# Ending a feed-forward layer and starting attention: earlier weight loads, sums written in place, keys moved

## The chip, the cores and the metric

The kernel runs on one core of a Trainium2 chip. The metric is the device time of one execution in microseconds (us); lower is better. A change of less than about 0.2% (3 us) is not told apart from none here.

## The reference

A "macaron" layer over x of shape (8, 512, 256), 4096 rows in all, in 32-bit floats:

```
x = x + 0.5 * ffn(layernorm(x))      # first feed-forward
x = x + attention(layernorm(x))      # 16 heads of 16, causal, over 512 rows
x = x + 0.5 * ffn(layernorm(x))      # second feed-forward, same weights

ffn(x) = silu(x @ w1) * (x @ w2) @ w3          # shared, hidden size 1024
       + sum over the top 2 of 16 experts of sigmoid-gate * (silu(x @ e1) * (x @ e2) @ e3)
attention: q, k, v = x @ Wq.T, x @ Wk.T, x @ Wv.T; softmax(q k / 4, causal) v; @ Wo.T
```

## The kernel before

The rows are handled in 8 chunks of 512 rows (`CHUNK`). One function, `feed_forward`, is called twice: for the first layer with `exact` false, for the second with `exact` true. Products are made in parts: each factor is split in a rounded high part and the rest (low part), and three of the four products are added.

In the first feed-forward the shared part of chunks 0 to 5 (`BEHIND` = 6) is computed first (`chunks_before`) and its result goes to DRAM (`dram.sh`). Then come 80 blocks of 128 rows sorted by expert (`steps`, `NB` = 80). Each block's result is evicted by VectorE (DVE) into one of four buffers `yr` and scattered to `outputs_by_choice` in DRAM by an indirect DMA that GpSimd (POOL) issues (line 1163). POOL issues the scatter of block i only when that of block i-2 has landed. Last comes the shared part of chunks 6 and 7 (`chunks_behind`), 16 steps s = 0 to 15, one for each tile of 128 hidden columns. This text calls them step 0 to step 15. A step is on TensorE (PE) "up(s)", 12 matmuls of L1712, then "down(s-1)", 12 matmuls of L1726 and L1730. Between them ScalarE (ACT) makes silu (L1273) and the high part of the hidden tile (L1277), and DVE the hidden tile (L1548) and its low part (L1565). up(s) also needs the hidden tile of step s-2, and down(s) both parts of step s.

In the shadow of these 16 steps the parts of all 8 chunks are added up:

- SyncE (SP) loads chunk c's two expert outputs (`load_y`, 1 MB, one of four buffers `yg`) and, for chunks 0 to 5, the shared result (`load_acc`, 0.5 MB, one of four buffers `acc`).
- ACT scales the second expert output by its gate at step `SCALE_AT[c]` = 3, 4, 5, 7, 8, 9, 10, 12 (L1227, in `ahead`).
- DVE adds the first, gated, and then the scaled second (`combine`, L1634 and L1631) at steps `COMBINE_AT`: chunk 0 at 3 and 4, chunk 1 at 4 and 5, chunk 2 at 5 and 6, chunk 3 at 7 and 8, chunks 4, 5 and 6 both at 10, 11 and 12, chunk 7 at 13 and 14. The second raises the semaphore `summed`.
- SP stores the sum (`store_out`) to `dram.x1`, and when it has landed reuses the `acc` buffer.

The start of attention is drawn into the same steps. Chunk 0's sum, loaded back from DRAM into `att.x1[:, 1]`, gets its layer norm statistics on DVE (step 9), the deviation on POOL (semaphore `a_dev`), the normalisation on ACT (step 11, `a_normed`), and is turned on PE (the "turn", L1786, after up(12) and before down(11)). ACT and DVE split it in parts (steps 13 and 14), and PE projects it with the weights `att.wqk` (the "projection", L1804, after down(14)), which have to be loaded back from DRAM together with `att.wv` (`a_w_in`). The projections' parts are laid out by DMAs into `att.qT` and `att.kT`, whose rows POOL has cleared before (`a_clear`).

What sets the order of the work is the program text of each engine. Each engine runs its own list in order, and SP's DMAs go through one queue in order. The attention tiles lie over the same memory as `yg`, `acc` and the experts' weights. In units of 1024 floats for each partition, `yg` lies at 0 to 8, `acc` at 8 to 12, `xb` at 12 to 14, `att.x1` at 16 to 18, `att.wqk` and `att.wv` at 20.5 to 23.5. Before, `att.kT` was at 0 to 8 (four slots of 2) and `att.qT` at 8 to 12. SP's list at the point of the change:

```python
            for c in range(AN):
                load_acc(c)
            for r in range(4):
                sp.wait_ge(y_st[r], 16 * (NB // 4))      # all scatters have landed
            for c in range(3):
                load_y(c)
                if c == 0 and not exact:
                    sp.wait_ge(y_ld[0], 16)
```

Of the kernel before, what the change touches and what calls it, by code (L numbers as in the profile page):

```python
# [6 lines left out]
P = 128  # L7
F32 = mybir.dt.float32
F32R = mybir.dt.float32r
# [406 lines left out]
def attention_memory(z, m):  # L416
# [6 lines left out]
    a.kT = m.sb("kT", [P, KEEP, GROUP, CHUNK], F32R)  # L423
    a.qT = m.sb("qT", [P, KEEP, GROUP // 2, CHUNK], F32R)

# [90 lines left out]
def lay_keys(eng, sem, att, s, parts, part, r):  # L516

    src, k = parts[:, part, :].bitcast(F32), att.kT[:, s].bitcast(F32)
# [58 lines left out]
def feed_forward(nc, z, g, dram, tag, x_src, pre, post, out):  # L578
# [27 lines left out]
    with ExitStack() as ctx:  # L606
# [80 lines left out]
        else:  # L687
# [8 lines left out]
            a_x_in = m.sems("a_x_in", 2)  # L696
# [118 lines left out]
        def _(sp):  # L815
# [242 lines left out]
            for c in range(AN):  # L1058
                load_acc(c)
            for r in range(4):  # L1060
                sp.wait_ge(y_st[r], 16 * (NB // 4))
# [9 lines left out]
            if not exact:  # L1071
                sp.dma_start(att.wqk[:].bitcast(F32).rearrange("p h k g n -> p (h k g n)"), dram.wqk).then_inc(a_w_in, 16)
                sp.dma_start(att.wv[:].bitcast(F32).rearrange("p h k n -> p (h k n)"), dram.wv).then_inc(a_w_in, 16)
            for c in range(NC):
                sp.wait_ge(summed, c + 1)
                if not exact and c == NC - 1:

                    sp.wait_ge(a_clear, 2)
                    sp.wait_ge(acc_st[0], 32)
# [5 lines left out]
                if c < BEHIND:  # L1085
                    store_out(c, acc[:, c % AN], acc_st[c % AN])
                    if c + GS < NC:
                        load_y(c + GS)
                    if c + AN < BEHIND:
                        sp.wait_ge(acc_st[c % AN], 16)  # L1090
                        load_acc(c + AN)
                        if not exact:
                            sp.dma_start(att.x1[:, 1 - c], out[bass.ds(c * CHUNK, CHUNK), :]
                                         .rearrange("(t p) d -> p t d", p=P)).then_inc(a_x_in[c], 16)
# [7 lines left out]
            else:  # L1102
                sp.wait_ge(a_x_in[1], 16)
# [3 lines left out]
        def _(pool):  # L1107
# [59 lines left out]
            if not exact:  # L1167
# [10 lines left out]

                pool.wait_ge(a_var, 1)
# [8 lines left out]

                pool.wait_ge(summed, 6)
                pool.sem_inc(g.held, 1)  # L1190
                for s in range(2):
                    nc.gpsimd.memset(att.kT[0:ROWS, s].bitcast(F32), 0.0).then_inc(a_clear, 1)

                pool.wait_ge(summed, 8)
                pool.sem_inc(g.held, 1)
                for s in range(2, KEEP):
                    nc.gpsimd.memset(att.kT[0:ROWS, s].bitcast(F32), 0.0)

        @block.scalar
        def _(act):  # L1200
# [19 lines left out]
            def ahead(s):  # L1220

# [7 lines left out]
                if s == 11:  # L1230
                    act.wait_ge(a_dev, 4)
                    for t in range(CT):
                        ins = nc.scalar.activation(att.xn[:, t, :], att.x1[:, 1, t, :], ACT.Identity,
                                                   bias=att.veps[:, 0, t:t + 1], scale=att.rstd[:, 0, t:t + 1])
                    ins.then_inc(a_normed, 1)
                elif s == 13:
# [3 lines left out]
                elif s == 15:  # L1240
# [6 lines left out]
                    act.wait_ge(acc_st[0], 32)  # L1247
# [64 lines left out]
        def _(dve):  # L1312
# [274 lines left out]
            def ahead(s):  # L1587

                if s == 9:
                    dve.wait_ge(a_x_in[0], 16)  # L1590
# [25 lines left out]
            def combine(c, k):  # L1616
# [12 lines left out]
                if k == 1 and not exact:  # L1629
                    dve.wait_ge(y_scaled, c + 1)  # L1630
                    v.tensor_tensor(base, base, yg[:, c % GS, :, 1, :], ALU.add).then_inc(summed, 1)  # L1631
# [312 lines left out]
def attention(nc, z, g, dram, att, mine, own, pre):  # L1944
# [75 lines left out]
    with ExitStack() as ctx:  # L2020
# [85 lines left out]
        def _(sp):  # L2106
# [6 lines left out]
            def lay_out(G):  # L2113
# [3 lines left out]
                q, k = qT[:, s].bitcast(F32), kT[:, s].bitcast(F32)  # L2117
# [63 lines left out]
            for part in range(2):  # L2181
# [6 lines left out]
            sp.dma_start(kT[ROWS:LAST_ROWS].bitcast(F32).rearrange("p s (g a) n -> p (s g) (a n)", a=2),  # L2188
                         pick[:].rearrange("p (o a) n -> p o (a n)", o=1).to_broadcast([2, KEEP * HG // 2, 2 * CHUNK])
                         ).then_inc(ones_in, 16)  # L2190
# [46 lines left out]
            sp.wait_ge(ones_in, 16)  # L2237
# [74 lines left out]
        def _(act):  # L2312
# [12 lines left out]
            def high(G):  # L2325
# [5 lines left out]
                if G < AHEAD:  # L2331

                    hi, lo = hiT[:, G % 2, :].bitcast(F32), loT[:, G % 2, :].bitcast(F32)
                    q, k = qT[:, G].bitcast(F32), kT[:, G].bitcast(F32)
# [446 lines left out]
```

## Time and profile before

| | |
|---|---|
| time, median of 3 runs | 1507.82 us (1505.16 to 1508.35) |
| time of the profiled execution | 1503.83 us |
| its span, first to last instruction | 1501.6 us |
| PE busy | 1427.6 us, 95% of the span |
| DVE, ACT, POOL busy | 64%, 44%, 39% |
| mean granted TensorE clock | 0.981 of full |

### The profile page before, as it was taken

What the parts mean: (1) busy time and instruction counts of PE and PEld (TensorE: products, weight loads), DVE (VectorE), ACT (ScalarE), POOL (GpSimd) and SP (SyncE); (2) the same over time, 40 slices, a digit from 0 to 9 for tenths busy, and PEclk for the clock granted to TensorE, in tenths of its full rate; (3) what the DMA queues carried; (4) which work ended last, traced back from release to release, by engine and by line L of the source; (5) the groups of instructions that cost most, each with busy time, mean ns of one, the idle gap of its engine ahead of it and who ended that gap; (6) DMA issues with size and microseconds to landing.
All of it is one profiled execution on the core that took longest, in us unless ns stands there. A gap on an engine that the chain in (4) does not pass through costs nothing. (4 is left out here: it accounts for less than half of the span.)

```text
span 1501.6 us, 28710 instructions
## 1 busy us (share of the span) xinstructions
PE 1427.6 (95%) x8840; PEld 1168.7 (78%) x8840; DVE 960.5 (64%) x2045; ACT 662.1 (44%) x1347; POOL 585.6 (39%) x832
## 2 busy tenths in 40 slices
PE   5899999999989978999999999889999899999998
PEld 2688878888878866767777767658888788888887
DVE  5678855565545756777677767536786455555566
ACT  4534444334333443656665565553322244343332
POOL 6528820233323023464465454321288333333100
PEclk9999999999999998999999999989999999999999
DMA  9897998534396856345554555445464634356941
GB/s 342 309 342 270 329 342 345 180 105 144 104 318 211 284 160 147 92 115 143 144 142 119 129 123 134 140 157 201 169 244 145 225 103 148 104 199 209 312 127 57
DMA packets 176533, 285.80 MB, mean 190 GB/s; under 512 B 20738, under 2 KB 125698, under 8 KB 176146
## 3 DMA queue, kind: packets, MB, share of 16 engines
q1 hardware_dynamic: 134642, 206.31, 43.6%
q0 software_dynamic: 19104, 56.64, 10.3%
q10 hardware_dynamic: 22656, 21.11, 4.8%
q8 instruction: 81, 1.33, 0.4%
q14 instruction: 50, 0.41, 0.1%
HBM read 144.20 MB, written 109.84 MB: 169 GB/s over the span
## 5 line engine op out<-in xcount | busy, mean ns | idle before, releaser
L1712 PE MATMUL f_bank<-f_xparts,f_sw 128*128 128x512 f32 x1536 | 375.9, 394 | 3.9 <-DVEq L1642 3.4
L1712 PEld LDWEIGHTS f_bank<-f_xparts,f_sw 128*128 128x128 f32 x1536 | 282.6, 190 | 59.8 <-DVEq L1642 4.3
L1163 POOL DMA_INDIRECT outputs_by_choice<-f_yr,f_home x160 | 153.6, 960 | 361.4 <-DVE f_yr L1666 306.2
L2438 DVE TENSOR_REDUCE at_mx<-at_ps 128x2 f32<-128x512 f32 (+2 forms) x352 | 213.3, 632 | 91.9 <-PE at_ps L2574 80.2
L2323 ACT ACTIVATE at_pT<-at_ps 128x512 f32<-128x512 f32 (+1 forms) x352 | 190.5, 560 | 70.0 <-PE at_ps L2596 63.7
L2251 POOL TENSOR_SCALAR_AFFINE_SELECT at_pT<-at_pT 128x128 f32<-128x128 f32 (+2 forms) x352 | 123.8, 358 | 206.4 <-ACT at_pT L2323 201.3
L1121 POOL DMA_INDIRECT rows_by_slot<-f_xq,slot x128 | 146.3, 1143 | 123.8 <-issue 72.3
L1655 DVE TENSOR_TENSOR f_sil<-f_sil,f_bank 128x256 f32<-128x256 f32 x160 | 67.4, 421 | 165.0 <-ACT f_sil L1297 152.5
L1548 DVE TENSOR_TENSOR f_hid<-f_sil,f_bank 128x512 f32<-128x512 f32 x128 | 87.8, 686 | 132.0 <-PE f_bank L1712 103.3
L2596 PE MATMUL at_ps<-fa_qT,fa_kT 98*128 98x256 f32 (+3 forms) x512 | 162.3, 370 | 6.9 <-DMA fa_qT<-at_mT 3.5
L1277 ACT CAST f_hparts<-f_hid 128x512 fp32r<-128x512 f32 x128 | 79.4, 620 | 202.0 <-DVE f_hid L1548 192.7
L1726 PE MATMUL f_bank<-f_sw,f_hparts 128*128 128x256 f32 x1024 | 147.3, 287 | 3.8 <-ACT f_hparts L1277 2.1
L1726 PEld LDWEIGHTS f_bank<-f_sw,f_hparts 128*128 128x128 f32 x1024 | 139.0, 192 | 13.5 <-ACT f_hparts L1277 5.3
L2574 PE MATMUL at_ps<-fa_kT,fa_qT 96*128 96x256 f32 (+2 forms) x448 | 147.4, 367 | 1.8 <-DVE at_mx L2438 1.8
L1273 ACT ACTIVATE f_sil<-f_bank 128x512 f32<-128x512 f32 x128 | 76.3, 596 | 143.6 <-PE f_bank L1712 119.4
L1297 ACT ACTIVATE f_sil<-f_bank 128x256 f32<-128x256 f32 x160 | 61.6, 385 | 173.5 <-PE f_bank L1846 170.5
L1565 DVE TENSOR_TENSOR f_hparts<-f_hid,f_hparts 128x512 fp32r<-128x512 f32 x128 | 88.4, 690 | 50.3 <-ACT f_hparts L1277 45.1
L2596 PEld LDWEIGHTS at_ps<-fa_qT,fa_kT 98*128 98x128 f32 x512 | 94.0, 195 | 24.4 <-ACT at_pT L2323 10.7
L1846 PE MATMUL f_bank<-f_ring,f_hparts 128*128 x320 | 100.8, 396 | 8.5 <-SPq L872 7.3
L1305 ACT CAST f_hparts<-f_bank 128x256 fp32r<-128x256 f32 x160 | 59.7, 373 | 84.5 <-PE f_bank L1822 78.8
L1846 PE MATMUL f_bank<-at_whi,f_hparts 128*128 x320 | 94.6, 418 | 0.0
L1846 PE MATMUL f_bank<-fa_whi,f_hparts 128*128 x320 | 93.9, 415 | 0.1
(262 smaller groups left out, 2433.0 us busy)
## 6 DMA issues: line engine op xcount, KB each, us to landing
f_ring<-weights_in_parts SPq DMA_DIRECT2D x32, 768.0 KB
weights_in_parts<-fa_whi SPq DMA_DIRECT2D x30, 768.0 KB, 9.1
f_rawx<-rows_by_slot ACTq DMA_DIRECT2D x152, 128.0 KB
at_whi<-weights_in_parts SPq DMA_DIRECT2D x16, 768.0 KB
fa_ew<-in_L_ffn_routed_w_dram SPq DMA_DIRECT2D x42, 256.0 KB, 5.6
rows_by_slot<-zero POOLq DMA_DIRECT2D x10, 1024.0 KB, 22.9
f_xq<-xn_rows POOLq DMA_DIRECT2D x32, 256.0 KB
fa_ew<-outputs_by_choice SPq DMA_DIRECT2D x8, 1024.0 KB, 9.1
```

Of the source, the lines that this page charges most:

```text
L1121: nc.gpsimd.indirect_dma_start(dram.xs, bass.IndirectOffsetOnAxis(ap=g.slot[:, at:at + 1], axis=0), xq[:, h % 4, t, :], None).then_inc(sca ...
L1163: nc.gpsimd.indirect_dma_start(dram.yk, bass.IndirectOffsetOnAxis(ap=home[:, i:i + 1], axis=0), yr[:, i % 4, :], None).then_inc(y_st[i % 4 ...
L1548: v.tensor_tensor(hid[:, j % 2], sil[:, j % 2, :], psB[j % 2][:, :], ALU.mult).then_inc(h_done, 1)
L1565: v.tensor_tensor(hparts[:, j % 2, 1], hid[:, j % 2], hparts[:, j % 2, 0], ALU.subtract).then_inc(h_lo, 1)
L1712: ins = pe.matmul(ps[j % 2][:, :], sw12[:, wp, k, w, j * P:(j + 1) * P], xparts[:, u, xp, k, :], start=(i == 0), stop=(i == 3 * KD - 1))
L1726: pe.matmul(psO[t], hparts[:, j % 2, 0, t * P:(t + 1) * P], sw3[:, wp, j, :], start=(j == 0 and wp == 0 and t % 2 == 0), stop=False, skip_ ...
L1846: ins = pe.matmul(rUp[r % 2][:, :], xsP[:, r % 2, xp, k * P:(k + 1) * P], w[:, bass.ds(base + k * 2 * RH, 2 * RH)], start=(n == 0), stop=( ...
L2251: p.affine_select(out=own, in_=own, compare_op=ALU.is_ge, fill=0.0, base=0, pattern=[[0, heads], [1, P]], channel_multiplier=-1).then_inc( ...
L2323: s_.activation(pT[:, i % SLOTS, 0:w], ps2[i % RING2][:, 0:w], ACT.Exp).then_inc(ex_done, 1)
L2438: v.tensor_reduce(own, ps1[i % RING1][:, 0:heads * w].rearrange("p (j a x) -> p j a x", a=min(heads, 2), x=w), AX.X, ALU.max).then_inc(mx_ ...
L2574: ins = pe.matmul(ps[:, j * w:(j + each) * w], qT[0:ROWS, G % KEEP, (h + j) // 2, qi * P:(qi + 1) * P], kT[0:ROWS, G % KEEP, h + j:h + j + ...
L2596: ins = pe.matmul(ps[:, j * w:(j + 1) * w], kT[0:LAST_ROWS, G % KEEP, h + j, ki * P:(ki + 1) * P], qT[0:LAST_ROWS, G % KEEP, (h + j) // 2, ...
```

## The change

Five things are done together:

1. The loads of `att.wqk` (1 MB) and `att.wv` (0.5 MB) are asked for when the last expert block is computed (`dn_done`), after the `acc` loads and before the wait for the scatters. Before they followed the fourth `load_y`.
2. DVE writes the sums of chunks 0 and 1 to `att.x1` and not over `acc`. They are stored from there. The two loads of these rows back from DRAM go, with their semaphores, and SP's two waits for a landed store before `load_acc(4)` and `load_acc(5)` go too.
3. In SP's list `load_y(c + 4)` and `load_acc(c + 4)` come ahead of the store of chunk c. For `load_y` this holds in the second feed-forward too.
4. The statistics of chunk 0 move from step 9 to step 7 on DVE, and the normalisation on ACT from the end of step 11 to step 9, ahead of that step's scaling.
5. The keys' four slots are split in two tiles with the queries between them: `k_early` at 0 to 4, `qT` at 4 to 8, `k_late` at 8 to 12. POOL clears slot 3 when the stores of chunks 2 and 3 have landed, slot 0 at `summed` 5, slot 1 at `summed` 6, slot 2 when the stores of chunks 4 and 5 have landed. Before it cleared two at `summed` 6 and two at `summed` 8. The rows of ones under the keys are filled by two DMAs, not one.

```diff
-    a.kT = m.sb("kT", [P, KEEP, GROUP, CHUNK], F32R)
+    a.k2 = [m.sb("k_early", [P, KEEP // 2, GROUP, CHUNK], F32R)]
     a.qT = m.sb("qT", [P, KEEP, GROUP // 2, CHUNK], F32R)
+    a.k2.append(m.sb("k_late", [P, KEEP // 2, GROUP, CHUNK], F32R))
+    a.kT = [half[:, s] for half in a.k2 for s in range(KEEP // 2)]
...
             for c in range(AN):
                 load_acc(c)
+            if not exact:
+
+                sp.wait_ge(dn_done, NB)
+                sp.dma_start(att.wqk[:].bitcast(F32).rearrange("p h k g n -> p (h k g n)"), dram.wqk).then_inc(a_w_in, 16)
+                sp.dma_start(att.wv[:].bitcast(F32).rearrange("p h k n -> p (h k n)"), dram.wv).then_inc(a_w_in, 16)
             for r in range(4):
                 sp.wait_ge(y_st[r], 16 * (NB // 4))
...
             load_y(3)
-            if not exact:
-                sp.dma_start(att.wqk[:].bitcast(F32).rearrange("p h k g n -> p (h k g n)"), dram.wqk).then_inc(a_w_in, 16)
-                sp.dma_start(att.wv[:].bitcast(F32).rearrange("p h k n -> p (h k n)"), dram.wv).then_inc(a_w_in, 16)
             for c in range(NC):
                 sp.wait_ge(summed, c + 1)
                 if not exact and c == NC - 1:
 
                     sp.wait_ge(a_clear, 2)
-                    sp.wait_ge(acc_st[0], 32)
                     sp.wait_ge(p_hi, 1)
...
                 if c < BEHIND:
-                    store_out(c, acc[:, c % AN], acc_st[c % AN])
                     if c + GS < NC:
                         load_y(c + GS)
                     if c + AN < BEHIND:
-                        sp.wait_ge(acc_st[c % AN], 16)
                         load_acc(c + AN)
-                        if not exact:
-                            sp.dma_start(att.x1[:, 1 - c], out[bass.ds(c * CHUNK, CHUNK), :]
-                                         .rearrange("(t p) d -> p t d", p=P)).then_inc(a_x_in[c], 16)
+                        store_out(c, att.x1[:, 1 - c], acc_st[c % AN])
+                    else:
+                        store_out(c, acc[:, c % AN], acc_st[c % AN])
...
+                pool.wait_ge(acc_st[2], 16)
+                pool.wait_ge(acc_st[3], 16)
+                pool.sem_inc(g.held, 1)
+                clear(3)
+                pool.wait_ge(summed, 5)
+                pool.sem_inc(g.held, 1)
+                clear(0)
                 pool.wait_ge(summed, 6)
                 pool.sem_inc(g.held, 1)
-                for s in range(2):
-                    nc.gpsimd.memset(att.kT[0:ROWS, s].bitcast(F32), 0.0).then_inc(a_clear, 1)
-
-                pool.wait_ge(summed, 8)
+                clear(1)
+                pool.wait_ge(acc_st[0], 32)
+                pool.wait_ge(acc_st[1], 32)
                 pool.sem_inc(g.held, 1)
-                for s in range(2, KEEP):
-                    nc.gpsimd.memset(att.kT[0:ROWS, s].bitcast(F32), 0.0)
+                clear(2)
...
             def ahead(s):
 
-
+                if s == 9:
+                    act.wait_ge(a_dev, 4)
+                    for t in range(CT):
+                        ins = nc.scalar.activation(att.xn[:, t, :], att.x1[:, 1, t, :], ACT.Identity,
+                                                   bias=att.veps[:, 0, t:t + 1], scale=att.rstd[:, 0, t:t + 1])
+                    ins.then_inc(a_normed, 1)
                 for c in range(NC):
                     if s == SCALE_AT[c]:
...
-                if s == 11:
-                    act.wait_ge(a_dev, 4)
...
-                elif s == 13:
+                if s == 13:
...
-                    act.wait_ge(acc_st[0], 32)
+                    act.wait_ge(summed, 7)
                     lay_other(act, g.laid[0], att, 0, att.p0, 0)
...
             def ahead(s):
 
-                if s == 9:
-                    dve.wait_ge(a_x_in[0], 16)
+                if s == 7:
+                    dve.wait_ge(summed, 1)
+                    dve.sem_inc(g.held, 1)
                     for t in range(CT):
                         v.bn_stats(att.stat[:, 0, t, :], att.x1[:, 1, t, :]).then_inc(a_st, 1)
...
                 if k == 1 and not exact:
                     dve.wait_ge(y_scaled, c + 1)
-                    v.tensor_tensor(base, base, yg[:, c % GS, :, 1, :], ALU.add).then_inc(summed, 1)
+                    total = att.x1[:, 1 - c] if c < 2 else base
+                    v.tensor_tensor(total, base, yg[:, c % GS, :, 1, :], ALU.add).then_inc(summed, 1)
                     return
...
-            sp.dma_start(kT[ROWS:LAST_ROWS].bitcast(F32).rearrange("p s (g a) n -> p (s g) (a n)", a=2),
-                         pick[:].rearrange("p (o a) n -> p o (a n)", o=1).to_broadcast([2, KEEP * HG // 2, 2 * CHUNK])
-                         ).then_inc(ones_in, 16)
+            for half in att.k2:
+                sp.dma_start(half[ROWS:LAST_ROWS].bitcast(F32).rearrange("p s (g a) n -> p (s g) (a n)", a=2),
+                             pick[:].rearrange("p (o a) n -> p o (a n)", o=1).to_broadcast([2, KEEP * HG // 4, 2 * CHUNK])
+                             ).then_inc(ones_in, 16)
```

## Rows read from the trace of the kernel before

**Rows 1.** Waits of all engines, 490 to 560 us: total, times, longest
```profile
ACT fa_ew L1227 <- DMA fa_ew<-outputs_by_choice: 10.4, 4, 3.9
```

**Rows 2.** Windows: busy of PE, PEld, DVE, ACT, POOL, then PEclk, DMA share, GB/s
```profile
481.00:488.00 7.00, 7.00 (x39) 6.04 (x38) 2.49 (x4) 2.16 (x4) 1.92 (x2) 1.00 1.03 355
488.00:491.90 3.90, 3.90 (x24) 3.41 (x24) 1.38 (x2) 0.94 (x3) 2.19 (x5) 1.00 0.11 40
...
500.00:536.00 36.00, 33.06 (x187) 28.31 (x185) 25.11 (x48) 18.04 (x39) 1.72 (x4) 1.00 1.07 365
...
536.10:542.90 6.80, 4.59 (x21) 4.60 (x22) 5.87 (x11) 4.86 (x11) 2.90 (x2) 0.50 0.36 121
```

**Rows 3.** Timeline of PE: start, duration (us), then what ended idle time before
```profile
521.54 2.91 PE L1712 MATMUL f_bank<-f_xparts,f_sw 128*128 128x512 f32 x12
524.28 1.11 PE L1726 MATMUL f_bank<-f_sw,f_hparts 128*128 128x256 f32 x8
...
525.72 2.91 PE L1712 MATMUL f_bank<-f_xparts,f_sw 128*128 128x512 f32 x12
529.41 1.21 PE L1726 MATMUL f_bank<-f_sw,f_hparts 128*128 128x256 f32 x8 [0.79 <-ACT f_hparts L1277]
...
538.31 1.97 PE L1786 MATMUL f_bank<-ident,fa_xn 128*128 128x128 f32 x8 [4.46 <-ACT fa_xn L1233]
...
555.35 2.91 PE L1804 MATMUL f_bank<-fa_xnT,fa_wqk 128*128 128x512 f32 x12
```

**Rows 4.** Timeline of ACT
```profile
525.80 1.71 ACT L1227 ACTIVATE fa_ew<-fa_ew,gate 128x256 f32<-128x256 f32 x4 [3.87 <-DMA fa_ew<-outputs_by_choice]
...
532.72 1.71 ACT L1227 ACTIVATE fa_ew<-fa_ew,gate 128x256 f32<-128x256 f32 x4 [3.35 <-DMA fa_ew<-outputs_by_choice]
...
536.18 2.07 ACT L1233 ACTIVATE fa_xn<-fa_x,fa_veps,fa_rstd 128x256 f32<-128x256 f32 x4
```

**Rows 5.** Timeline of SP's queue
```profile
491.89 8.60 SPq L1055 DMA_DIRECT2D fa_ew<-outputs_by_choice  x4
500.54 2.74 SPq L1072 DMA_DIRECT2D fa_wqk<-ueries_and_keys_in_parts  x1
...
515.88 0.51 SPq L1055 DMA_DIRECT2D fa_ew<-outputs_by_choice  x1
```

**Rows 6.** Timeline of DVE
```profile
505.56 0.69 DVE L1548 TENSOR_TENSOR f_hid<-f_sil,f_bank 128x512 f32<-128x512 f32 x1 [0.48 <-ACT f_sil L1273]
...
515.35 1.67 DVE L1634 SCALAR_TENSOR_TENSOR fa_ew<-fa_ew,gate 128x256 f32<-128x256 f32 x4
...
522.57 1.40 DVE L1592 BATCH_NORM_STATS2 fa_stat<-fa_x 128x6 f32<-128x256 f32 x4
524.11 0.39 DVE L1596 BATCH_NORM_AGGREGATE fa_mv<-fa_stat 128x2 f32<-128x6 f32 x4
528.02 0.69 DVE L1548 TENSOR_TENSOR f_hid<-f_sil,f_bank 128x512 f32<-128x512 f32 x1 [3.53 <-ACT f_sil L1273]
529.39 0.69 DVE L1565 TENSOR_TENSOR f_hparts<-f_hid,f_hparts 128x512 fp32r<-128x512 f32 x1 [0.69 <-ACT f_hparts L1277]
530.00 1.67 DVE L1634 SCALAR_TENSOR_TENSOR fa_ew<-fa_ew,gate 128x256 f32<-128x256 f32 x4
531.70 1.23 DVE L1631 TENSOR_TENSOR fa_ew<-fa_ew 128x1024 f32<-128x1024 f32 x1
...
553.13 1.28 DVE L1601 TENSOR_TENSOR fa_xnT<-f_bank,fa_xnT 128x512 fp32r<-128x512 f32 x2
```

**Rows 7.** Timeline of POOL: the last scatters
```profile
477.67 0.96 POOL L1163 DMA_INDIRECT outputs_by_choice<-f_yr,f_home  x1 [1.60 <-DVE f_yr L1666]
482.99 0.96 POOL L1163 DMA_INDIRECT outputs_by_choice<-f_yr,f_home  x1 [4.36 <-DVE f_yr L1666]
484.78 0.96 POOL L1163 DMA_INDIRECT outputs_by_choice<-f_yr,f_home  x1 [0.83 <-DMA outputs_by_choice<-f_yr,f_home]
489.42 0.96 POOL L1163 DMA_INDIRECT outputs_by_choice<-f_yr,f_home  x1 [3.67 <-DMA outputs_by_choice<-f_yr,f_home]
```

More of the change, by code:

```diff
@@ L516, in lay_keys @@
 def lay_keys(eng, sem, att, s, parts, part, r):
-    src, k = parts[:, part, :].bitcast(F32), att.kT[:, s].bitcast(F32)
+    src, k = parts[:, part, :].bitcast(F32), att.kT[s].bitcast(F32)
     for a in range(2):
@@ L695, in feed_forward @@
             a_w_in = m.sem("a_w_in")
-            a_x_in = m.sems("a_x_in", 2)
             y_scaled = m.sem("y_scaled")
@@ L1102, in _ @@
             else:
-                sp.wait_ge(a_x_in[1], 16)
                 sp.wait_ge(a_w_in, 32)
@@ L1177, in _, with clear @@
                                         base=0, pattern=[[0, GROUP], [-1, P]], channel_multiplier=1)
+                def clear(s):
+                    nc.gpsimd.memset(att.kT[s][0:ROWS].bitcast(F32), 0.0).then_inc(a_clear, 1)
                 pool.wait_ge(a_var, 1)
@@ L1229, in ahead @@
                         ins.then_inc(y_scaled, 1)
-                if s == 11:
-                    act.wait_ge(a_dev, 4)
[L1232 to L1235, printed above, removed]
-                elif s == 13:
+                if s == 13:
                     for k in range(KD):
@@ L2116, in lay_out @@
                 hi, lo = hiT[:, u, :].bitcast(F32), loT[:, u, :].bitcast(F32)
-                q, k = qT[:, s].bitcast(F32), kT[:, s].bitcast(F32)
+                q, k = qT[:, s].bitcast(F32), kT[s].bitcast(F32)
                 def put(dst, src):
@@ L2236, in _ @@
             sp.wait_ge(xnT2_st, 16 * (NB_ - 1))
-            sp.wait_ge(ones_in, 16)
+            sp.wait_ge(ones_in, 32)
         @block.gpsimd
@@ L2333, in high @@
                     hi, lo = hiT[:, G % 2, :].bitcast(F32), loT[:, G % 2, :].bitcast(F32)
-                    q, k = qT[:, G].bitcast(F32), kT[:, G].bitcast(F32)
+                    q, k = qT[:, G].bitcast(F32), kT[G].bitcast(F32)
                     act.wait_ge(hi_done, G + 1)
@@ L2574, in score1 @@
                     ins = pe.matmul(ps[:, j * w:(j + each) * w], qT[0:ROWS, G % KEEP, (h + j) // 2, qi * P:(qi + 1) * P],
-                                    kT[0:ROWS, G % KEEP, h + j:h + j + each, k0 * P:k0 * P + w], start=(j == 0),
+                                    kT[G % KEEP][0:ROWS, h + j:h + j + each, k0 * P:k0 * P + w], start=(j == 0),
                                     stop=(not masked and j + each == heads), skip_group_check=True)
@@ L2589, in score2 @@
                 if i == 0:
-                    pe.wait_ge(ones_in, 16)
+                    pe.wait_ge(ones_in, 32)
                 if n == 0:
@@ L2595, in score2 @@
                 for j in range(heads):
-                    ins = pe.matmul(ps[:, j * w:(j + 1) * w], kT[0:LAST_ROWS, G % KEEP, h + j, ki * P:(ki + 1) * P],
+                    ins = pe.matmul(ps[:, j * w:(j + 1) * w], kT[G % KEEP][0:LAST_ROWS, h + j, ki * P:(ki + 1) * P],
                                     qT[0:LAST_ROWS, G % KEEP, (h + j) // 2, ki * P:CHUNK], start=(j == 0),
```

## The prediction

> **What bounds the kernel now.** I read the page first: TensorE (PE) is busy for 95% of the span, so only an idle stretch of PE, or one at the lower clock, can be won. The change touches the last 16 steps of the first feed-forward and the first instructions of attention. The waits of this stretch come next. ACT waits four times, 10.4 us in all, for a loaded expert output before it scales it [rows 1]. The windows say why: from 500 to 536 us the DMA engines are full and move 365 GB/s [rows 2]. So a transfer asked for in this time lands late, and the loads stand behind whatever SP asked for earlier.
>
> PE's timeline shows what that costs. A step takes 4.18 us when nothing is missing: up 2.74, down 1.44 (521.54, 524.28, 525.72) [rows 3]. PE stands 0.79 us before down(10) and 4.46 us before the turn [rows 3]. ACT's timeline names the chain: the scaling of chunk 5 starts at 525.80 after 3.87 us of waiting, that of chunk 6 at 532.72 after 3.35 us, and only then comes the normalisation at 536.18, for which the turn waits [rows 4]. After this idle time the granted clock is 0.50, the 1.2 GHz level, from 536.1 to 542.9, with PE busy for 4.6 us of it [rows 2].
>
> How much can be won at most? From up(11) at 525.72 to the projection at 555.35 are 29.6 us [rows 3]. They hold five ups, five downs and the turn: 5 x 4.18 = 20.9, and for the turn about 0.9 (estimated as half of the 1.97 that it took at the lower clock [rows 3], less the overlap). That leaves 7.8 us: 5.25 idle, the rest the lower clock. This is the ceiling.
>
> **Part by part, 1: the DMAs.** Out of the full stretch go two loads back of 0.5 MB (2.9 us at 365 GB/s [rows 2], a MB being 1024 KB) and the 1.5 MB of weights, which stood at 500.54 ahead of the later loads [rows 5]: 4.3 us. Chunk 5's output, which SP asked for at 515.88 because it stood behind a wait for a landed store [rows 5], is asked for when chunk 1 is summed, near 510. From 500.5 on the queue holds in order y1 to y3, y4, acc4, store 0, y5, acc5, store 1, store 2, y6: 9.5 MB, 27.3 us. Chunk 5's output, after 6 MB, lands at about 518 to 520 instead of 525.8, chunk 6's at about 528 instead of 532.7. ACT then comes to them at 525.7 and 529.3 (below), so neither is waited for, with 1.5 us to spare at chunk 6. The idle time and the lower clock go. But two new chains are next.
>
> **2: ACT and DVE, steps 7 to 10.** DVE's step 7 gets the statistics, 1.40 + 0.39 = 1.8 us [rows 6]. Chunk 3's first addition starts at 515.35 and takes 1.6 [rows 6], so step 8's hidden tile starts at 518.8. From a hidden tile's start to the end of its high part on ACT are 1.37 us (528.02 to 529.39, where the low part starts) [rows 6]: 520.1. From the start of a scaling to the next hidden tile are 2.2 us (525.80 to 528.02) [rows 4, 6]: step 9's tile starts at 522.3, its high part is done at 523.7. Now the normalisation, 2.0 [rows 4], stands ahead of chunk 5's scaling: 525.7, and 2.2 later, at 527.9, step 10's tile starts. Before it was 528.02 [rows 6]. So what DMA gave, the two moved pieces take back up to here: PE waits about half a microsecond in step 8 and as much in step 10.
>
> **3: DVE, steps 10 to 14.** Steps 10, 11 and 12 each hold tile to low part 1.37, low part 0.61, first addition 1.70, second 1.15 (issue to issue; the recorded durations overlap the next start by 0.08) [rows 6]: 4.83, more than PE's 4.18. Step 13 has no second addition: 3.6. Step 14 has 1.37 + 0.61 + 1.15 and the split of the turned chunk, 1.28 less 0.08 [rows 6]: 4.3. Sum 3 x 4.83 + 3.6 + 4.3 = 22.4. From 527.9 this gives 550.3 for the low parts, and the projection starts there; PE itself would be ready at about 549.2. Before it started at 555.35 [rows 3]. Gain with everything else in place: 5.0 us of the ceiling of 7.8.
>
> **4: the weights' new place.** This is the term against the change. SP asks for 1.5 MB at about 481.5, when the last block is done. Its queue is still full from the loads before, and the DMA engines are until 488 (share 1.03 in 481 to 488, 0.11 in 488 to 491.9) [rows 2]. At 365 GB/s the new 4.3 us fill 487.7 to 492.0, exactly the free stretch. In it runs the last scatter, issued at 489.42, and SP asks for the first output at 491.89, when it has landed: 2.5 us [rows 5, 7]. With full engines a scatter takes longer: that of 477.67 releases the one at 484.78 after 7.1 us, that of 482.99 the one at 489.42 after 6.4, which is 1.7 us after the engines came free [rows 7]. So the last scatter lands between 491.9 (not touched) and, if also the one before is held until the new load is through, 492.0 + 1.7 + 2.5 = 496.2. I take that it is issued on time and lands 1.7 us after the engines come free, as the one of 482.99 did, because the rows hold no scatter nearer to it: 493.6, a delay of 1.7 us. Bounds 0 and 4.3. Is the delay hidden? No: the second output is asked for when the first has landed, ACT waits for both [rows 1], DVE's tile of step 5 at 505.56 comes after 0.48 us of idle time behind ACT [rows 6], and from there DVE has nothing idle but the 0.69 waits inside each step, so steps 5 to 8 and the chain above move by the whole delay.
>
> The Trainium skill ("DMA: Bandwidth & Descriptors", section "Queues, rings and completion order") says that each DMA engine takes its queues in turn, but a whole packet of some 9 to 17 descriptors from one before it goes to the next. By that rule a scatter waits for long pieces of the weights at each turn, which speaks for the far bound; the 7.1 us above agree with it, and the sum would be 5.0 less 4.3.
>
> **5: the rest.** The loads of y ahead of the stores cost nothing in the second feed-forward: PE is not idle once in its last 100 us by the timeline. The four clears on POOL are the same four of 1.8 us, spread over a time in which POOL is idle, and a clear is needed only behind the projection. If that cover were gone, the layout would wait 1.8 us; I take 0. The second DMA for the rows of ones costs SP's queue 0.6 to 0.8 us at attention's start, where SP waits for the first high part anyway: 0. Sums written to another tile cost the same. Where the lower clock of attention's start falls is not known beforehand; bounds -1 and +1.
>
> **Sum.** 5.0 - 1.7 = 3.3 us. Against the profiled execution's own 1503.83 (span 1501.6 and 2.2 around it) that is 1500.5. That execution is 4.0 us under the median of 1507.82, so for the median I forecast 1504.5.
>
> **The rivals.** A: the weights are hidden entirely, because the scatter's small writes get their turns. For it speaks that one of 477.67 did land with the engines full until 488 [rows 2, 7]. Then 5.0 us: 1502.8. B: the last but one scatter is held as well, and the delay is 4.3: gain 0.7, time 1507.1, nothing to be measured. C, the other side: the last two scatters each take the 7.1 us of the row or more: the last but one lands at 490.1, the last at 497.2 or later. From a delay of 5 us (496.9) the change loses, and with PE standing over 4 us in steps 4 and 5 the lower clock comes too, for 6.8 us as at 536.1 [rows 2], of which half of PE's 4.6 us are lost, 2.3. At a delay of 6 us: 6 + 2.3 - 5.0 = 3.3 slower, 1511.1. Against it: the engines have nothing to move but the weights after 487.7. D: the two moved pieces and DVE's load are not in the way, because DVE's additions overlap better than issue to issue. Then the ceiling less the delay, 7.8 - 1.7 = 6.1: 1501.7. Against it stands that the 4.83 us steps are plain sums of rows. E: the idle time does not go, because the outputs still land late. It would need the queue over 1.5 us behind my count at chunk 6. Each microsecond more costs one: a gain of 1, 1506.8.
>
> **How the numbers follow.** The forecast, a gain of 2 to 4.5, gets 0.50; A 0.15; B 0.15; C 0.07; D 0.05; E 0.08. A change under 0.2% (3.0 us) can't be told from none here. The forecast's part above 3.0 (0.32 of its 0.50), A and D give faster 0.52. Slower by over 0.2% is C and 0.01 of E: 0.08. The rest is 0.40. The range leaves C and the far half of D out: gains of 6.8 to -0.5, 1501.0 to 1508.3.
>
> **What would show it.** Right: PE without idle time over 1.5 us from 492 to the projection, the granted clock 1.0 there; the first output asked for 1 to 2.5 us later after the end of the blocks than now; the normalisation ahead of the turn by 5 us or more; hidden tiles of steps 10 to 13 some 4.8 us apart; the projection 3 to 4 us earlier, right behind DVE's low parts and not behind down(14). Wrong: the scatters not touched (A) or both held (B, C), an ACT wait for chunk 6's output (E), tiles 4.2 us apart (D).

## The result, and the profile after

| | before | after |
|---|---|---|
| median, 10 runs of each, in turns on one chip | 1505.6 us (1499.42 to 1508.61) | 1496.3 us (1492.05 to 1501.58) |
| ratio after / before, 95% | | 0.9949 (0.9934 to 0.9965) |
| profiled execution: span | 1501.6 us | 1494.6 us |
| mean granted TensorE clock | 0.981 | 0.981 |

Faster by 0.51%, 7.7 us of 1505.6 (5.3 to 9.9 by the interval). I had forecast 3.3 us, and a range from 6.8 faster to 0.5 slower. Against the 1507.82 us on which the forecast was built the ratio gives 1500.1, the runs themselves 1496.3: both are below the range's 1501.0.

Single executions differ by some 5 us for reasons that have nothing to do with the change: the first products of the 16 steps (up(0) and up(1), one row of L1720 x24 after) start between 472.8 and 483.6 us in the profiles of this study, and what lies behind the start of attention lasts 934 to 941 us. So I compare the stretch of the change by times counted from the start of up(0), called F here: 481.15 before, 480.67 after. The rows of before for F and for the first scaling, which the rows ahead of the prediction do not hold:

```profile
481.15 5.63 PE L1712 MATMUL f_bank<-f_xparts,f_sw 128*128 128x512 f32 x24
```

```profile
497.79 1.71 ACT L1227 ACTIVATE fa_ew<-fa_ew,gate 128x256 f32<-128x256 f32 x4 [1.20 <-DMA fa_ew<-outputs_by_choice]
```

| us after F | before | after | gain |
|---|---|---|---|
| SP asks for the first expert output | 10.74 | 12.94 | -2.2 |
| ACT starts the first scaling | 16.64 | 18.43 | -1.8 |
| projection starts | 74.20 | 70.75 | 3.45 |
| attention's first product | 86.30 | 78.77 | 7.53 |

The first three rows are what the prediction is about, and 3.45 us is what it said, 3.3. Another 4.1 us appear between the projection and attention, where it had nothing at all. In the spans it adds up: F is 0.5 earlier, the stretch 7.5 shorter, the rest 1.0 longer, in all the 7.0 us between 1501.6 and 1494.6.

The timeline of PE after, start, duration, then idle time before (answers to [rows 3]):

```profile
480.67 5.61 PE L1720 MATMUL f_bank<-f_xparts,f_sw 128*128 128x512 f32 x24
...
508.05 1.21 PE L1734 MATMUL f_bank<-f_sw,f_hparts 128*128 128x256 f32 x8 [0.87 <-ACT f_hparts L1283]
...
534.62 1.03 PE L1794 MATMUL f_bank<-ident,fa_xn 128*128 128x128 f32 x8
...
551.42 3.01 PE L1812 MATMUL f_bank<-fa_xnT,fa_wqk 128*128 128x512 f32 x12 [0.77 <-DVE fa_xnT L1608]
554.27 1.11 PE L1734 MATMUL f_bank<-f_sw,f_hparts 128*128 128x256 f32 x8
555.23 0.64 PE L1738 MATMUL f_bank<-f_sw,f_hparts 128*128 128x256 f32 x4
559.44 0.94 PE L2641 MATMUL at_psX<-fa_wv,fa_xnT 128*128 128x256 f32 x6 [3.58 <-PEq L2754]
```

The 4.46 us before the turn are gone, and the projection waits 0.77 us for DVE's low parts, as forecast. All of PE's idle time in the steps is 2.6 us in six pieces, none above 0.87. The last row is attention's first product, behind the end of the feed-forward's block. The same row of the kernel before, which the rows ahead of the prediction do not hold:

```profile
567.45 1.62 PE L2632 MATMUL at_psX<-fa_wv,fa_xnT 128*128 128x256 f32 x6 [7.76 <-PEq L2745]
```

In both kernels PE is idle behind L2745 or L2754, the clean-up between one block and the program's next, but 7.76 us before and 3.58 after. There are the missing 4.2 us.

The timeline of ACT after (answers to [rows 4]; L1239 are the scalings, L1232 the normalisation):

```profile
499.10 1.71 ACT L1239 ACTIVATE fa_ew<-fa_ew,gate 128x256 f32<-128x256 f32 x4 [3.01 <-DMA fa_ew<-outputs_by_choice]
...
504.44 1.71 ACT L1239 ACTIVATE fa_ew<-fa_ew,gate 128x256 f32<-128x256 f32 x4 [1.77 <-DMA fa_ew<-outputs_by_choice]
...
524.76 2.08 ACT L1232 ACTIVATE fa_xn<-fa_x,fa_veps,fa_rstd 128x256 f32<-128x256 f32 x4
526.74 1.69 ACT L1239 ACTIVATE fa_ew<-fa_ew,gate 128x256 f32<-128x256 f32 x4
...
530.19 1.71 ACT L1239 ACTIVATE fa_ew<-fa_ew,gate 128x256 f32<-128x256 f32 x4
```

ACT's waits for loaded outputs are two, 4.8 us, where they were four, 10.4 [rows 1]; chunks 5 and 6 are not waited for.

SP's queue and POOL's scatters after (answer to [rows 5, 7]), first SP, then POOL:

```profile
480.87 2.06 SPq L1064 DMA_DIRECT2D fa_wqk<-ueries_and_keys_in_parts  x1
482.97 0.63 SPq L1065 DMA_DIRECT2D fa_wv<-values_in_parts  x1
493.61 11.31 SPq L1056 DMA_DIRECT2D fa_ew<-outputs_by_choice  x5
```

```profile
484.79 0.96 POOL L1162 DMA_INDIRECT outputs_by_choice<-f_yr,f_home  x1 [0.30 <-issue]
490.63 0.96 POOL L1162 DMA_INDIRECT outputs_by_choice<-f_yr,f_home  x1 [4.88 <-DMA outputs_by_choice<-f_yr,f_home]
```

The last scatter is issued 9.96 us after F where it was 8.27, having waited 4.88 us for an earlier one to land, and lands 3.0 us after its issue (493.61 - 490.63) where it took 2.5.

DVE's hidden tiles of steps 10 to 13 after (answer to [rows 6]), and the windows of the steps (columns as in [rows 2]):

```profile
528.95 0.69 DVE L1554 TENSOR_TENSOR f_hid<-f_sil,f_bank 128x512 f32<-128x512 f32 x1 [3.37 <-ACT f_sil L1279]
533.77 0.68 DVE L1554 TENSOR_TENSOR f_hid<-f_sil,f_bank 128x512 f32<-128x512 f32 x1
538.59 0.68 DVE L1554 TENSOR_TENSOR f_hid<-f_sil,f_bank 128x512 f32<-128x512 f32 x1
543.41 0.68 DVE L1554 TENSOR_TENSOR f_hid<-f_sil,f_bank 128x512 f32<-128x512 f32 x1
```

```profile
488.00:490.00 2.00, 2.00 (x10) 1.65 (x9) 0.46 (x1) 0.60 (x1) 0.00 (x0) 1.00 0.99 404
490.00:492.00 2.00, 2.00 (x17) 1.88 (x16) 0.74 (x2) 0.71 (x2) 1.22 (x3) 1.00 0.49 201
```

```profile
481.00:492.00 11.00, 11.00 (x62) 9.57 (x61) 3.93 (x7) 3.69 (x7) 3.15 (x5) 1.00 0.96 354
...
500.00:525.00 25.00, 23.87 (x132) 19.94 (x131) 20.47 (x43) 14.13 (x32) 2.26 (x4) 1.00 1.06 349
525.00:551.00 26.00, 24.96 (x145) 21.06 (x143) 19.10 (x33) 13.66 (x29) 7.23 (x4) 1.00 0.40 130
```

The tiles are 4.82 us apart. The weights keep the DMA engines full until about 491 (share 0.99 in 488 to 490, 0.49 in 490 to 492), where they had been free from 488 [rows 2]; the granted clock stays at 1.00, the 2.4 GHz level.

Now the block's end. These are the instructions of one line, the end of the block, by engine: name, count, duration in ns (least, median, greatest), then when they start. First before, then after (with two entries, the start given first and POOL's greatest duration are the first feed-forward's; ACT's least is the first feed-forward's):

```profile
L606 POOLq DRAIN  x2: 9998/11179/12360, 553.4 to 1403.0; - x2
...
L606 ACTq DRAIN  x2: 396/522/649, 561.2 to 1493.7; - x2
L606 SPq DRAIN  x2: 7/8/9, 561.3 to 1501.4; - x2
...
L606 ACTq EVENT_SEMAPHORE  x2: 17/17/17, 565.9 to 1501.5; - x2
```

```profile
L608 POOLq DRAIN  x2: 10000/10329/10658, 541.7 to 1396.1; - x2
...
L608 ACTq DRAIN  x2: 396/522/647, 557.4 to 1486.8; - x2
L608 SPq DRAIN  x2: 7/30/53, 557.4 to 1494.4; - x2
...
L608 ACTq EVENT_SEMAPHORE  x2: 17/17/17, 557.9 to 1494.6; - x2
```

```profile
553.36 3.56 POOL L1197 MEMSET fa_kT<- 96x2048 f32 x2 [9.81 <-DVE fa_ew L1631]
```

```profile
538.83 1.81 POOL L1179 MEMSET fa_k_early<- 96x2048 f32 x1 [3.01 <-DVE fa_ew L1639]
541.75 1.81 POOL L1179 MEMSET fa_k_late<- 96x2048 f32 x1 [1.11 <-DMA x_rows<-fa_ew]
```

The last two clears before stood behind the last sum, since their slots lay over `yg`. With the late keys over `acc`, the last clear stands behind a landed store. In both kernels the drain ends 8.8 us after the last clear does (565.76 - 556.92 and 552.40 - 543.56).

### The profile page after: what moved, and what is told of

It is laid out like the page before. It is cut to its first block and busy times, and to the rows that moved or that the text cites. A ratio compares the mean times of both kernels' runs of the same rounds, so it can differ in the third digit from the quotient of the medians.

```text
span 1494.6 us, 28676 instructions
## 1 busy us (share of the span) xinstructions
PE 1430.4 (96%) x8806; PEld 1169.2 (78%) x8840; DVE 956.9 (64%) x2045; ACT 661.6 (44%) x1347; POOL 585.1 (39%) x832
## 3 DMA queue, kind: packets, MB, share of 16 engines
q0 software_dynamic: 19104, 56.64, 10.4%
## 5 line engine op out<-in xcount | busy, mean ns | idle before, releaser
L1720 PE MATMUL f_bank<-f_xparts,f_sw 128*128 128x512 f32 x1536 | 375.3, 394 | 3.3 <-DVEq L1650 2.3
L1720 PEld LDWEIGHTS f_bank<-f_xparts,f_sw 128*128 128x128 f32 x1536 | 282.6, 190 | 58.3 <-DVEq L1650 3.3
L1663 DVE TENSOR_TENSOR f_sil<-f_sil,f_bank 128x256 f32<-128x256 f32 x160 | 67.5, 422 | 163.8 <-ACT f_sil L1303 157.9
L1734 PE MATMUL f_bank<-f_sw,f_hparts 128*128 128x256 f32 x1024 | 146.4, 285 | 2.2 <-ACT f_hparts L1283 1.8
L2605 PE MATMUL at_ps<-fa_qT,fa_k_late 98*128 98x512 f32 (+3 forms) x256 | 82.5, 377 | 5.3 <-DMA fa_qT<-at_mT 2.6
L1738 PE MATMUL f_bank<-f_sw,f_hparts 128*128 128x256 f32 x512 | 82.8, 284 | 3.0 <-DVE f_hparts L1571 2.4
L2605 PE MATMUL at_ps<-fa_qT,fa_k_early 98*128 98x512 f32 (+3 forms) x256 | 81.2, 368 | 2.6 <-DMA fa_qT<-at_mT 2.2
```

What stands on the lines that cost most here:

```text
L1720: ins = pe.matmul(ps[j % 2][:, :], sw12[:, wp, k, w, j * P:(j + 1) * P], xparts[:, u, xp, k, :], start=(i == 0), stop=(i == 3 * KD - 1))
L1734: pe.matmul(psO[t], hparts[:, j % 2, 0, t * P:(t + 1) * P], sw3[:, wp, j, :], start=(j == 0 and wp == 0 and t % 2 == 0), stop=False, skip_ ...
L1738: ins = pe.matmul(psO[t], hparts[:, j % 2, 1, t * P:(t + 1) * P], sw3[:, 0, j, :], start=False, stop=(j == z.JS - 1), skip_group_check=True)
L2605: ins = pe.matmul(ps[:, j * w:(j + 1) * w], kT[G % KEEP][0:LAST_ROWS, h + j, ki * P:(ki + 1) * P], qT[0:LAST_ROWS, G % KEEP, (h + j) // 2, ...
```

## The experiments

All ratios are against the kernel before, run beside them. Times are from F as above.

| kernel | first output asked | projection | attention | gap at the block's end | PE idle in the steps | ratio (95%) |
|---|---|---|---|---|---|---|
| before | 10.74 | 74.20 | 86.30 | 7.76 | 5.25 | |
| b_clears | 10.93 | 75.34 | 83.26 | 3.59 | 5.99 | 0.9975 (0.9955 to 0.9995) |
| b_drain | 10.98 | 74.74 | 82.65 | 3.58 | 6.17 | 0.9980 (0.9961 to 0.9999) |
| after | 12.94 | 70.75 | 78.77 | 3.58 | 2.6 | 0.9949 (0.9934 to 0.9965) |
| a_again | 13.41 | 71.16 | 79.17 | 3.54 | 2.5 | 0.9952 (0.9931 to 0.9974) |
| a_late_pool | 12.74 | 70.38 | 85.53 | 10.69 | 1.9 | 0.9991 (0.9969 to 1.0014) |
| a_weights_last | 11.32 | 70.48 | 78.50 | 3.57 | 2.0 | 0.9935 (0.9909 to 0.9961) |
| a_stats_old | 12.87 | 68.37 | 76.29 | 3.58 | 1.25 | 0.9922 (0.9895 to 0.9950) |
| a_stats_old_2 | 12.69 | 68.03 | 75.95 | 3.58 | 1.1 | 0.9920 (0.9888 to 0.9952) |
| a_sums_only | 11.18 | 69.38 | 77.29 | 3.57 | 2.35 | 0.9938 (0.9917 to 0.9959) |
| a_both | 10.70 | 66.44 | 74.35 | 3.57 | 0 | 0.9924 (0.9896 to 0.9951) |
| a_both_2 | 11.19 | 67.48 | 75.40 | 3.58 | 0.5 | 0.9907 (0.9875 to 0.9939) |

**b_clears**: the kernel before with only the keys' tiles, the clears and the waits that belong to them changed.

```diff
-    a.kT = m.sb("kT", [P, KEEP, GROUP, CHUNK], F32R)
+    a.k2 = [m.sb("k_early", [P, KEEP // 2, GROUP, CHUNK], F32R)]
     a.qT = m.sb("qT", [P, KEEP, GROUP // 2, CHUNK], F32R)
+    a.k2.append(m.sb("k_late", [P, KEEP // 2, GROUP, CHUNK], F32R))
...
-                pool.wait_ge(summed, 8)
+                pool.wait_ge(acc_st[0], 32)
+                pool.wait_ge(acc_st[1], 32)
                 pool.sem_inc(g.held, 1)
-                for s in range(2, KEEP):
-                    nc.gpsimd.memset(att.kT[0:ROWS, s].bitcast(F32), 0.0)
+                clear(2)
```

> Kernel before with the keys split in two tiles and the four clears at their new times, nothing else. Theory POOL-exit (the block's end waited for GpSimd, whose drain ends 8.8 us after its last clear, 565.8 in the kernel before): the projection stays where it was (74.2 us after the first up-product of chunk 6), the gap of TensorE between the two blocks falls from 7.8 to about 3.6 us, the kernel is 4 us faster. Rival DMA-only (everything came from the loads and from the removed waits): gap 7.8, kernel unchanged within 1 us.

The gap falls to 3.59 us, and the projection is not earlier (1.1 us later in this execution). Attention starts 3.0 us earlier, the time is 0.25% shorter. So the layout and the clears alone bring what the prediction missed, and nothing of what it counted.

**a_late_pool**: the kernel after, with one tiny clear of four floats for each partition, of a part of a tile that nothing uses there, put late on POOL. It leaves the data flow as it is.

```diff
                 clear(2)
+                pool.wait_ge(p_lo, 2)
+                pool.sem_inc(g.held, 1)
+                nc.gpsimd.memset(att.veps[:, 1, :], 0.0)
```

> Kernel after with one more GpSimd instruction at the very end of the block: a clear of 4 floats per partition in a scratch tile, behind the low parts of the projections (about 555.8). Theory POOL-exit with a drain of fixed length: the drain ends 8.8 us after it, at about 564.8, the gap of TensorE between the blocks grows from 3.6 to about 10.5 us, the kernel is 7 us slower than after, about equal to before. Rival, the drain's length goes with the size of the clears before it: the gap grows by under 1 us.

Its rows: the clear on POOL, POOL's drain at the block's end (the greatest duration is the second feed-forward's), and attention's first product on PE.

```profile
549.08 0.11 POOL L1207 MEMSET fa_veps<- 128x4 f32 x1 [12.41 <-DVE fa_p L1616]
```

```profile
L608 POOLq DRAIN  x2: 8938/9470/10002, 549.1 to 1400.2; - x2
```

```profile
559.70 1.62 PE L2644 MATMUL at_psX<-fa_wv,fa_xnT 128*128 128x256 f32 x6 [10.69 <-PEq L2757]
```

0.11 us of work cost 7.1 us of gap (10.69 - 3.58). Of the 0.51% by which the kernel after is faster 0.09% is left, with an interval (0.9969 to 1.0014) that includes no change. The drain takes 8.94 us, 8.8 past the end of a clear sixteen times shorter. So it is not the size of the clears that the block's end waits for, but a fixed length behind POOL's last instruction.

**b_drain**: the kernel before, its clears as late as they were, with one more instruction on POOL behind the masks.

```diff
                 nc.gpsimd.affine_select(out=maskq[:], in_=maskq[:], compare_op=ALU.is_ge, fill=MASK, ...
+                pool.drain()
```

> Kernel before with one explicit drain on GpSimd right behind the last scatter and the masks, at about 492 us, where GpSimd is idle for 30 us. Theory: the 8.8 us of the drain at the block's end stand for the indirect DMAs issued since the last drain; this one takes them, the one at the end is short (0.7 us, as in the attention block), the gap of TensorE between the blocks falls to 3.6 and the kernel is 4 us faster. Rival: any drain on GpSimd in this block takes 8.8 us from the last instruction, the gap stays 7.8 and nothing is gained.

The added drain (line L1178) and the one at the block's end, whose first entry is the first feed-forward's:

```profile
L1178 POOLq DRAIN  x1: 9485/9485/9485, 490.1 to 490.1; - x1
```

```profile
L606 POOLq DRAIN  x2: 3599/6798/9997, 552.1 to 1400.3; - x2
```

```profile
552.09 3.56 POOL L1198 MEMSET fa_kT<- 96x2048 f32 x2 [8.94 <-DVE fa_ew L1632]
```

The early drain ends at 499.6, 8.8 us after the mask at 490.72; the late one is over with the clears at 555.7, with nothing behind them. The gap is 3.58, as expected, and the kernel 0.20% faster, 3.0 us where 4 were expected (interval 0.2 to 5.9). The 8.8 us are paid once, at the first drain behind the scatters, early or late. In the block of attention, on whose POOL no indirect DMA runs, the drain of the kernel after takes 0.7 us:

```profile
L2028 POOLq DRAIN  x1: 724/724/724, 979.0 to 979.0; - x1
```

The second feed-forward of the kernel after has no clears at its end; there POOL's last instruction is a scatter, and its drain (from 1396.1 for 10.0 us, line L608 above) again ends 8.8 us behind it:

```profile
1396.35 0.96 POOL L1162 DMA_INDIRECT outputs_by_choice<-f_yr,f_home  x1 [3.86 <-DMA outputs_by_choice<-f_yr,f_home]
```

That it is the indirect DMAs since the last drain that make its length fits all of these, but no run here takes the scatters away or changes their number, and POOL asks for plain DMAs too in a feed-forward block and for none in attention's; this part is argued, not shown.

**a_stats_old** and **a_stats_old_2** (the same kernel on another chip): the kernel after with the statistics at step 9 and the normalisation at step 11, as they had been.

```diff
-                if s == 9:
-                    act.wait_ge(a_dev, 4)
...
+                if s == 11:
+                    act.wait_ge(a_dev, 4)
...
-                if s == 7:
+                if s == 9:
                     dve.wait_ge(summed, 1)
```

> Kernel after with chunk 0's statistics back at step 9 and its normalisation back at step 11. Theory: the two pieces at steps 7 and 9 are what pushes the hidden tiles of steps 8 and 10 late; without them hidden tile 10 starts 3 us earlier, VectorE enters its crowded steps with slack, and the projection starts about 2.5 us earlier than in after (68 to 68.5 us after the first up-product of chunk 6). Rival: the early normalisation is what makes the turn come on time; back at step 11 the turn waits again, the projection comes as late as in after or later.

> The kernel with only statistics and normalisation at their old steps, weights asked for at the blocks' end, once more: projection 68.4 us after the first up-product of chunk 6, 1 to 2 us slower than the kernel beside it, 10 us faster than before.

The projection starts at 68.37 and 68.03, where after, a_again and a_late_pool have 70.38 to 71.16: 2.0 to 3.1 us earlier, 2.4 between a_stats_old and after. Step 10's hidden tile starts 45.26 us after F and not 48.28, the 3 us expected. The two moved pieces are a loss: they are early for a turn that PE reaches in step 12, and in steps 7 to 10 they stand ahead of scalings and tiles that PE does wait for. They were moved back together, so how the loss divides between them stays open. The expectation of a_stats_old_2 missed in its times: by the whole time a_stats_old_2 is not slower than a_both_2 beside it (medians 1488.3 and 1488.7 us), and it is 12 us faster than before, not 10.

**a_weights_last**: the kernel after with the two weights' DMAs behind the store of chunk 3.

```diff
-                sp.wait_ge(dn_done, NB)
-                sp.dma_start(att.wqk[:] ...
-                sp.dma_start(att.wv[:] ...
...
+                    if not exact and c == 3:
+                        sp.dma_start(att.wqk[:] ...
+                        sp.dma_start(att.wv[:] ...
```

> Kernel after with the attention weights asked for behind the load of chunk 7's outputs and the store of chunk 3, when the queue has nothing more to load. Theory: in the kernel after the weights hold up the last scatter, so the first output is asked for 1.7 to 2.2 us late; here it comes at the old place (10.7 us after the first up-product of chunk 6), all of steps 4 to 14 move with it and the projection starts 1.7 us earlier than in after (69.0 us after that up-product instead of 70.75). Rival: the delay is hidden by the slack of the steps, the projection stays at 70.75.

The first output is asked for 1.6 us earlier, so the delay of the scatters does go. But its landing takes longer (the first scaling starts 6.6 us behind the request, 5.5 after), and the projection comes only 0.3 us earlier than in after, less than the 0.4 by which after and a_again differ. The expectation of the whole delay was wrong.

**a_again**, **a_sums_only**, **a_both**: the kernel after unchanged, on the chip of the other two; with a_stats_old's edit and the weights at their old place behind `load_y(3)`; with a_stats_old's and a_weights_last's edits.

> The kernel after once more, as the measure for the kernels beside it: 7 to 8 us faster than before, projection 70.4 to 70.8 us after the first up-product of chunk 6, gap between the blocks 3.6 us.

> Kernel after with the weights asked for at their old place behind the fourth load of outputs, and statistics and normalisation at steps 9 and 11: of the change only the sums written in place, the order of SP's list and the clears are left. Theory of the full queue: the 4.3 us of the weights come back ahead of chunks 4 to 7, the outputs of chunk 6 land 2 to 3 us too late, ScalarE waits for them once, the projection starts 1 to 2.5 us later than with the weights out of the way (68.4), at 69.5 to 71. Rival: the two loads back and the waits for landed stores were all that mattered, the projection stays at 68.4.

> Kernel after with the weights asked for last and with statistics and normalisation back at steps 9 and 11. If the two effects seen alone add up (0.3 and 2.4 us of the projection's time), the projection starts about 68.1 us after the first up-product of chunk 6 and the kernel is 2.5 to 3 us faster than after. Rival: with the steps no longer late the full delay of the last scatter counts, and the projection starts at 67.0 or earlier.

> The kernel with weights last and statistics at their old steps once more, on the same chip as the one beside it. If its steps are free of idle time whenever it runs, the projection starts 66.4 to 67.5 us after the first up-product of chunk 6 again, and the kernel is 11 to 12 us faster than before (ratio 0.992). Rival: the 66.44 of the first look came from the late end of the blocks in that execution, and in another one the first output lands late as it did with only the weights last; then 68 us and no difference to the kernel beside it.

a_sums_only and b_clears differ by the sums written in place, with the loads back and the waits that this saves, and by the order of SP's list alone: the projection starts at 69.38 and 75.34. These 6 us are the largest piece of what the change gained; the whole time agrees (ratios of 0.9938 and 0.9975).

a_sums_only also shows what the weights at 500 us cost. Its timelines of ACT and PE:

```profile
527.25 1.71 ACT L1231 ACTIVATE fa_ew<-fa_ew,gate 128x256 f32<-128x256 f32 x4 [2.71 <-DMA fa_ew<-outputs_by_choice]
```

```profile
532.85 1.09 PE L1792 MATMUL f_bank<-ident,fa_xn 128*128 128x128 f32 x8 [1.40 <-ACT fa_xn L1237]
```

Chunk 6's output lands late again, and the turn waits 1.40 us: the chain of the kernel before, in small. Its 69.38 stand against 68.2 with the weights at the blocks' end (the mean of 68.37 and 68.03) and 66.4 and 67.5 with the weights last. So their new place brings about 1.2 us over the old one, and the place behind chunk 3's store another 0.7 to 1.8, once the statistics are out of the way. These are sizes from one or two executions each, and two executions of one kernel differ by up to 1.0 us here (66.44 and 67.48); what the rows show is the wait. In a_both PE is not idle at all in the steps, in a_both_2 for 0.5 us. The projection and attention's first product of a_both_2:

```profile
542.07 2.91 PE L1810 MATMUL f_bank<-fa_xnT,fa_wqk 128*128 128x512 f32 x12
...
549.99 0.95 PE L2639 MATMUL at_psX<-fa_wv,fa_xnT 128*128 128x256 f32 x6 [3.58 <-PEq L2752]
```

The projection of a_both at 66.44 is 7.76 us before that of the kernel before; the prediction's ceiling was 7.8. Attention starts 11 to 12 us earlier than before and 3.4 to 4.4 earlier than after, earliest of all kernels here. That this kernel beats after is shown by the stretch and not by the whole time, where its 0.9907 and 0.9924 have intervals that overlap with that of after (0.9934 to 0.9965); a_stats_old, with 0.9922 and 0.9920, isn't told apart from it either.

Of the four expectations of this group none held in full. a_again's projection came at 71.16, above its 70.4 to 70.8. a_sums_only waited for chunk 6 as expected, with 69.38 just before its 69.5 to 71. a_both's sum of 68.1 was wrong and its rival right: the two moves together bring 4.3 us (70.75 - 66.44), or 3.3 by a_both_2, where one by one they brought 0.3 and 2.4. In a_both_2 the projection came at 67.48, at the edge of what was expected, while the first scaling was late (17.67, near the 17.96 of a_weights_last), as its rival had it.

## Why the prediction was wrong

- **Part 5, "the rest", failed.** It said: "The four clears on POOL are the same four of 1.8 us, spread over a time in which POOL is idle, and a clear is needed only behind the projection. If that cover were gone, the layout would wait 1.8 us; I take 0." That holds for the data: nobody waits for a clear. But they were POOL's last work in the block, and the block's end waits for POOL. A term was missing: who ends the block. Both numbers lay in the trace of before: ACT and SP are done at 561.6, the engines go on at 565.9. It is worth 4.2 us (7.76 - 3.58), and 3.3 + 4.2 = 7.5 is the measured 7.5 to 7.7. None of the five rivals held it; each ended its count at the projection. What makes the drain last 8.8 us stays open.
- **Part 1 right in its mechanism, with a wrong sum.** The queue that it lists holds 8.5 MB, 24.4 us, not 9.5 and 27.3. So by its own working chunk 6's output lands near 525, over 4 us ahead of ACT and not 1.5; nothing in the forecast's sum hangs on it. Chunks 5 and 6 are not waited for, the clock stays at 1.00, PE's idle time in the steps falls from 5.25 to 2.6 us. Rival E is out.
- **Parts 2 and 3 right.** Counted with the delay of 1.7 and F 0.5 earlier, step 10's tile was forecast at 527.9 + 1.7 - 0.5 = 529.1, measured 528.95; steps of 4.83 us, measured 4.82; low parts at 551.5, the projection starts at 551.42 and waits for them. Rival D is out. The half microsecond in step 8 and in step 10 is there too: up(9) to up(10) take 4.63 us (518.47 to 523.10 in PE's timeline) and up(11) to up(12) 4.62 (527.25 to 531.87) in place of 4.18. That the moved pieces eat part of the gain is shown: 2.4 us.
- **Part 4 near in size, wrong in how, and its fit in part luck.** The delay was taken as 1.7 us between 0 and 4.3 (its "1.7 us after the engines came free" counts from 487.7; from the 488 of [rows 2] it is 1.4). The first output is asked for 2.2 us later, ACT starts on it 1.8 us later. But the prediction had the last scatter issued on time. It is issued 1.7 us later, held by an earlier one, which is half of rival B, and takes 0.5 us more to land. By their sizes rival A (not touched) and B and C (held fully) are out. All twelve profiles bear the delay out: SP asks for the first output 10.7 to 11.3 us after F in the seven kernels without the early weights, 12.7 to 13.4 in the five with them. At ACT it shrinks: its first scaling starts at 16.5 to 18.1 and at 18.0 to 18.8, by the means 0.9 us apart. The profile of before, on which the forecast was built, is one of the two earliest (16.64). So that 3.45 came within 0.2 us of 3.3 is in part luck. PE's largest idle piece, 0.87 us before down(5), which the prediction did not name, goes with that start: it is absent in before and a_both (16.64 and 16.45) and 0.98 us in a_again (18.76). The Trainium skill ("DMA: Bandwidth & Descriptors", section "Queues, rings and completion order") lets a whole packet of one queue pass before the next has its turn; of the far bound of 4.3 us that the prediction tied to it, the trace shows 2.2. And the delay is not the term's net worth: taking it away alone gave 0.3 us (a_weights_last).
- **The cost of the moved loads and the second DMA for the ones: 0**, as far as it can be told; behind attention's start the profiles with the change last 934.9 to 941.4 us, that of before 934.1, with 6.3 us between after and a_again, two executions of the same kernel.

## What to carry to other kernels

Count on to the next barrier. At the end of a block every engine waits for the slowest to finish, so before costing an edit at nothing because its engine is idle, look at the end-of-block instructions of all engines: who comes last, by how much, and does the edit touch that engine's last instruction. On GpSimd behind indirect DMAs, keep the last instruction 9 us ahead of the time at which the other engines are done, or pay the drain early with one of your own. And work that is moved ahead of its need lands on some engine's list in front of something that is needed: the statistics and the normalisation two steps earlier cost 2.4 us that the earlier load had bought.

## What the runs showed of the hardware

- GpSimd's first drain behind its indirect DMAs lasts 8.8 us past its last instruction, the same when that is the last scatter itself and when it comes 2 us or 51 to 66 us behind it, whatever it is (a mask of 0.64 us, a clear of 0.11, of 1.8). A second drain in the same block takes none of it, and one in a block without such DMAs 0.7 us. The Trainium skill ("VectorE: DVE Perf Modes", section "The DRAIN you can't avoid") describes drains in a program's preamble and postamble, about 12 ns long on all 5 engines. Those at the ends of a kernel's own blocks are others, and the figure does not carry over to them: here SP's are 7 to 53 ns, ACT's at the ends of the feed-forwards 396 to 649 ns and GpSimd's up to 12.4 us, of which 3.6 us are the clears before it.
- The last scatter lands 2.47 or 2.48 us after its issue in the seven kernels without the early weights, and 2.98 to 3.99 us after it in the five that ask for the 1.5 MB of weights before it. The scatter two places before it, issued while the DMA engines are full, took 6.4 us in the kernel before and 7.1 in the kernel after.
- From the request of the first expert output to ACT's start on it, 5.9 us pass in the kernel before and 6.9 in b_clears, which asks for the same bytes in the same order; over all kernels it is 5.3 to 6.9. So of a request made 1.6 us earlier (a_weights_last) 0.5 us reached ACT.
- Between the end of the feed-forward's last product and attention's first, 3.54 to 3.59 us pass in every kernel whose block is ended by ACT and SP.
